# Attention: where the shares of values, the maxima made ahead and the cut of the maxima stand

## The reference

```
x = x + tanh(g) * attention(layernorm(x), context)      # 16 heads of 16 numbers
x = x + tanh(g) * mixture_of_experts(layernorm(x))      # 8 experts, top 2
x = x + tanh(g) * attention(layernorm(x), context)      # again 16 heads
x = x + tanh(g) * (fp8(layernorm(x)) @ fp8(weight).T + bias)
```

## Time and profile before

| what | us |
| --- | --- |
| median of three runs | 1636.0 |
| the profiled execution, its own time | 1635.6 |
| its span, first to last instruction | 1633.6 |
| TensorE matmul busy | 1458.6 (89%) |
| VectorE busy | 1288.9 (79%) |
| ScalarE busy | 1010.4 (62%) |
| GpSimd busy | 636.8 (39%) |
| attention of layer 0, first scores to last values | 115.7 to 439.6 |
| attention of layer 1 | 1203.5 to 1528.3 |
| exponentials, 1024 (L1141) | 550.7 |
| reductions of pairs, 416 (L349) | 488.3 |
| reductions of single banks, 136 (L356) | 87.0 |

### The profile page before, as it was taken

How to read it: one execution, slowest core, us unless ns; L and a number is a source line. 1 busy time by engine, 2 the same in 40 slices (tenths; PEclk the granted TensorE clock), 3 DMA queues, 4 the chain that set the end, 5 groups by cost and what they waited for, 6 DMA issues and landing times. The chain is left out here.

```text
span 1633.6 us, 29384 instructions
## 1 busy us (share of the span) xinstructions
PE 1458.6 (89%) x10909; PEld 950.2 (58%) x10910; DVE 1288.9 (79%) x2135; ACT 1010.4 (62%) x1748; POOL 636.8 (39%) x957
## 2 busy tenths in 40 slices
PE   7989999999994399999999999879979999999845
PEld 6853333333484299999999999745523333333534
DVE  6889999999576766666665564379889999999687
ACT  5648999999741144444444444335549999989544
POOL 4315555556021234443432332255325555553120
PEclk9989999999995599999999999979979999999977
DMA  9974565555262123222222221168845555554103
GB/s 286 329 212 106 128 128 128 128 129 129 74 246 90 46 65 97 65 82 94 71 80 90 75 78 36 45 201 284 250 94 124 129 125 127 126 126 105 35 0 103
DMA packets 118748, 198.64 MB, mean 122 GB/s; under 512 B 29568, under 2 KB 63680, under 8 KB 117584
## 3 DMA queue, kind: packets, MB, share of 16 engines
q1 hardware_dynamic: 83840, 111.22, 22.3%
q0 software_dynamic: 33360, 83.94, 20.6%
q10 hardware_dynamic: 1408, 1.61, 0.3%
HBM read 117.77 MB, written 77.87 MB: 120 GB/s over the span
## 5 line engine op out<-in xcount | busy, mean ns | idle before, releaser
L1141 ACT ACTIVATE i_room<-a_ring 128x512 f32<-128x512 f32 x1024 | 550.7, 606 | 61.7 <-PE a_ring L1077 14.4
L349 DVE TENSOR_REDUCE logit<-a_ring 128x2 f32<-128x1024 f32 x416 | 488.3, 1217 | 3.7 <-PE a_ring L343 3.7
L1088 PE MATMUL a_pout<-i_room,values 128*17 128x256 f32 x4096 | 309.5, 386 | 3.2 <-ACT i_room L1141 1.7
L1799 ACT ACTIVATE e_full<-e_pH,b1T 128x320 f32<-128x320 f32 x256 | 135.0, 527 | 246.4 <-PE e_pH L1740 235.7
L1748 PE MATMUL e_pY<-fc_w,e_hid_hi 128*128 128x512 f32 x640 | 237.2, 407 | 0.5 <-DVE e_hid_lo L1852 0.5
L1077 PE MATMUL a_ring<-i_qk 64*128 64x512 f32 x768 | 193.9, 502 | 19.3 <-DVE logit L349 16.2
L1749 PE MATMUL e_pY<-fc_w,e_hid_lo 128*128 128x256 f32 x640 | 179.8, 281 | 0.0
L1077 PEld LDWEIGHTS a_ring<-i_qk 64*128 64x128 f32 x768 | 72.6, 186 | 183.3 <-DVE logit L349 134.2
L1088 PEld LDWEIGHTS a_pout<-i_room,values 128*17 128x17 f32 x4096 | 74.6, 95 | 175.8 <-ACT i_room L1141 137.1
L1860 POOL DMA_INDIRECT w<-normed,slot_get x80 | 83.6, 1045 | 225.7 <-PE fc_turned L1725 199.6
L1852 DVE TENSOR_TENSOR e_hid_lo<-e_full,e_hid_hi 128x640 fp32r<-128x640 f32 x128 | 119.6, 934 | 55.4 <-ACT e_hid_hi L1808 55.4
(11 more groups left out here) (337 smaller groups left out, 2576.2 us busy)
## 6 DMA issues: line engine op xcount, KB each, us to landing
ks<-i_room SPq DMA_DIRECT2D x64, 256.0 KB, 4.3
outs<-a_osb SPq DMA_DIRECT2D x64, 256.0 KB, 3.4
qs<-i_room SPq DMA_DIRECT2D x60, 256.0 KB, 5.3
fc_raw<-in_L_ffn_fc_w SPq DMA_DIRECT2D x15, 1024.0 KB, 5.4
i_qk<-ks POOLq DMA_DIRECT2D x84, 128.0 KB, 3.4
i_qk<-qs POOLq DMA_DIRECT2D x84, 128.0 KB, 3.6
BIG<-outs SPq DMA_DIRECT2D x64, 128.0 KB
ytok<-r_zeros SPq DMA_DIRECT2D x8, 1024.0 KB, 10.3
```

What stands on the lines that cost most here:

```text
L349: return e.tensor_reduce(nmax[:, :].rearrange("p (x y t) -> p x y t", x=2, y=2)[:, :, p, t], pair[:, :, :], AX.X, ALU.max, negate=True)
L1088: mm = e.matmul(pout[32 * h:32 * h + VW, at], v[:, b * TPB + t, g * HG + h, :], pexp[t][:, h, at], start=(t == 0 and half == 0), stop=(t = ...
L1141: e.activation(pexp[t][:, 2 * p + hh, :], score_bank(n * U + i, hh), ACT.Exp).then_inc(exped, 1)
L1799: e.activation(full[s % 2][:, h * WIDE:(h + 1) * WIDE], pH[h][:, 0:WIDE], ACT.Silu, bias=S.b1T[:, n * KF + f:n * KF + f + 1]).then_inc(act, 1)
```

## The change

Three things, in both layers. (1) Maxima run 16 units ahead, two whole groups, instead of 14; so the stages before an attention make two more units each, and the parts of a group's maxima are due beside the second reduction of the next group. (2) The parts are made in two pieces: the cast behind the next group's first reduction, the difference and the transpose behind its second. (3) Every step has one share of values: unit 5 in step 0, unit 6 in step 1, and unit 7 in step 2, there between the scores and the maxima. ScalarE's copy moves from behind both exponentials of unit 1 to between the two of unit 2.

```diff
-AHEAD = 2 * UNITS - 2
+AHEAD = 2 * UNITS
-LATE_VALUES = (UNITS - 3,), (UNITS - 2, UNITS - 1)
...
                         score_unit(n, i)
+                        if n and i == VALUE_LAG - 1:
+                            values(n - 1, (U - 1) // 2, (U - 1) % 2)
                         if s + 1 < PAIRED:
                             if s:
                                 e.wait_ge(exped, 2 * s - 1)
...
                         elif n and i < VALUE_LAG - 1:
-                            for v_unit in LATE_VALUES[i]:
-                                values(n - 1, v_unit // 2, v_unit % 2)
+                            late = U - VALUE_LAG + i
+                            values(n - 1, late // 2, late % 2)
...
                         for hh in range(2):
                             e.activation(pexp[t][:, 2 * p + hh, :], score_bank(n * U + i, hh), ACT.Exp).then_inc(exped, 1)
-                        if i == 1 and n:
-                            take_outputs(n - 1)
+                            if n and i == VALUE_LAG - 1 and hh == 0:
+                                take_outputs(n - 1)
...
+                def cut_maxima(n, part):
+                    halves, whole = max_halves(nparts[n % 2]), max_whole(nmax[n % 2])
+                    if part == HI:
+                        if (n + 1) * U > AHEAD:
+                            e.wait_ge(reduced, (n + 1) * U - AHEAD)
+                        e.tensor_copy(halves[:, :, 0, :], whole).then_inc(cut, 1)
+                    else:
+                        e.wait_ge(cut, 2 * n - 1)
+                        e.tensor_tensor(halves[:, :, 1, :], whole, halves[:, :, 0, :], ALU.subtract).then_inc(cut, 1)
+
                 def turn_maxima(n):
-                    halves, whole = max_halves(nparts[n % 2]), max_whole(nmax[n % 2])
-                    e.wait_ge(reduced, (n + 1) * U - AHEAD)
-                    e.tensor_copy(halves[:, :, 0, :], whole).then_inc(cut, 1)
-                    e.wait_ge(cut, 2 * n - 1)
-                    e.tensor_tensor(halves[:, :, 1, :], whole, halves[:, :, 0, :], ALU.subtract).then_inc(cut, 1)
                     if n >= 3:
                         e.wait_ge(mrow[(n - 2) % G], moved(n - 2))
                     e.wait_ge(cut, 2 * n)
...
                 for m in range(AHEAD, NG * U):
                     reduce(m)
-                    if m % U == U - 1:
-                        turn_maxima(m // U)
+                    if m >= 2 * U and m % U == 0:
+                        cut_maxima(m // U - 1, HI)
+                    if m >= 2 * U and m % U == 1:
+                        cut_maxima(m // U - 1, LO)
+                        turn_maxima(m // U - 1)
+                for part in (HI, LO):
+                    cut_maxima(NG - 1, part)
+                turn_maxima(NG - 1)
```

## The result

The changed kernel takes **1650.5 us** (median of 4 runs, 1648.2 to 1651.7) against 1635.2 for the kernel before in the same job: ratio 1.0089, 95% interval [1.0077, 1.0101]. On a second chip, later, it took 1646.8 (5 runs) against 1635.4: 1.0074 [1.0061, 1.0087]. So it is slower, by 11 to 15 us, where 8 were predicted. Its profiled execution is 1648.2 us with a span of 1646.1, which is 12.5 over the span of before.

What follows compares the result with a forecast made beforehand. TensorE was taken to set the pace of most steps, waiting for VectorE once a group. Terms 1.9 + 4.5 − 0.4 − 0.3 + 2.4 = +8.1 us on the profiled 1635.6; forecast 1644.0 us, range 1633 to 1651.

Steps and rivals of the forecast that it cites:

- The stall at unit 4: Each group: 2.80 us from T2 (start of scores 2) to T4, where TensorE needs 2.44; 0.36 us stall, +1.9 us overall.
- rival 1: The new stall at unit 4 does not bind and all steps are even: −13.3 us, 1623; chance 0.13.
- rival 2: The stall at unit 4 is smaller, 0.25 or 0.16 us: 1638 or 1632; chance 0.16.
- The cut in two pieces: At scores 3 of each group: the cast no longer waits for the reduction before it, and the old wait is gone.
- the 19.5 us "at stake": Both attentions: period 10.10 against 9.76 for eight even steps, 0.34 us a group, about 58 times.
- The copy: ScalarE's copy between unit 2's exponentials starts at T2 (start of scores 2) + 1.12, ends at 1.72; cost 0.
- Rival 4: Even steps come, but the copy ends late and binds, 0.1 to 0.2 us a group: about 1653; chance 0.04.
- The stages: Ends of the stages before each attention: two more units made, 2 × 1.13 us in each layer, +4.5 us.
- Loads: Twice in each layer a load in which GpSimd pauses lands 0.6 us late for its maxima: 4 × 0.6 = +2.4 us.
- rival 3: Loads late in every group; at a wait of 0.3 us a group, +17 more: 1661; chance 0.07.
- The first group: First group of an attention: the cast leaves the chain before scores 3; −0.3 us (0 to −0.8), in layer 0 alone.
- The tail: End of each attention: two steps lose their maxima, 0.99 instead of 1.22 us; −0.4 taken, at most 0.9 in all.

Runs made afterwards that it cites:

- experiment 4: The kernel before with only the maxima's parts made in two pieces (14 units ahead, old shares and copy): 1632.6 us, ratio 0.9987.
- experiment 7: The kernel before with only the even shares and the copy's new place (14 ahead, parts in one piece): 1639.0 us, ratio 1.0026.
- experiment 3: The changed kernel with the old shares and old copy place, 16 ahead and two pieces kept: 1643.4 us, ratio 1.0044.
- Experiment 9: The changed kernel with both pieces of the maxima's parts one reduction later, still 16 ahead: 1642.0 us, ratio 1.0041.
- experiment 10: The changed kernel with GpSimd's cast of the identity moved behind its last load: 1644.8 us, ratio 1.0052.
- experiment 1: The changed kernel with maxima 14 units ahead again, even shares, copy and two pieces kept: 1639.6 us, ratio 1.0023.
- experiment 8: The kernel before with two pieces and the copy between unit 2's exponentials, 14 ahead, old shares: 1640.0 us, ratio 1.0022.
- experiment 2: The changed kernel with unit 7's share behind the maxima of unit 2 instead of ahead of them: 1643.7 us, ratio 1.0049.

## Why the prediction was right or wrong

The direction and the mechanism were right and the range held the time; the sum was 4.4 us short of the profiled execution's 12.5, and 7 short of the first median. Of the 4.4 the loads are 3.0, the first groups 1.5 and the period 0.9; the stages, the tails and the untouched stages came out 0.3 to 0.4 lower each. The first median lies 0.5 us inside the upper end of the range, which had the loads doubled. Step by step:

**The stall at unit 4, right in place and size.** Predicted 0.43 + 0.56 + 0.54 + 1.22 + 0.05 = 2.80 from T2 to T4; measured 0.42, 0.56, 0.55, then 1.28 to the scores, 2.81. The choice of 0.54 over 0.43 for maxima behind values is what the trace shows (297.06 to 297.61), so the weight load of the maxima is paid openly there, as the rule of the Trainium skill (TensorE: Matmul & The Clock Gate, Part 3, The mechanism) had it. The trace does not bear out the rule's other half. In the kernel before the maxima stand behind scores, which use the same rows of the array, and yet the row of their weight load starts while the scores run, which last from 289.77 to 290.26 (the page also names a background weight buffer, of which no run here tells):

```profile
289.88 0.19 PEld L343 LDWEIGHTS a_ring<-i_qk 64*128 64x128 f32 x2
```

The period came out at 10.13, as predicted, and rivals 1 and 2 fall. The term was 2.8 us for 1.9, since the old period was 10.08 to 10.09 and not 10.10: the mean of the copies had in it one step of layer 1 that was 0.4 us long.

**The cut in two pieces, right but never seen.** Its gain is real, 2.3 us a layer (experiment 4), and the even shares hide all of it (experiment 7). It is also small: with the old shares, once the old wait is gone, the copy behind the double share holds the group at 10.01 us (experiments 3 and 4), far from the 9.76 that the 19.5 us "at stake" were reckoned from.

**The copy, right**: at T2 + 1.12 as worked out (296.08 to 297.20), no wait. Rival 4 falls.

**The stages, right**: +4.2 for +4.5.

**Loads, right in kind, wrong in size**: 5.4 for 2.4. The step that failed is "lands 3.7 later, at 259.2 ... late by 0.6". The row of before was taken over as if landings were a property of the load. They depend on what SyncE issues beside it. The text said that SyncE's DMAs "are issued no later", and took that for harmless; they were issued 0.3 to 0.35 us earlier (3.70 behind scores 7 instead of 4.05), next to the load's last pieces, which then took 4.1 us. A paused load's step lost 1.2 us for the predicted 0.6: 0.4 us and more of the excess is the later landing, and a step loses 0.2 us more than its load is late. Three smaller late steps, 0.7 together, were not foreseen. (The "covered by 2.4 us" was a misreading without effect: 2.4 is the length of the two steps; the room was 1.9.) Experiment 9 shows that moving them away takes the late steps out. The direction of the whole, four late loads, not one in every group, was right, and rival 3 falls.

**The first group, wrong in sign**: "the cast leaves that chain: −0.3", measured +0.6 in each layer. The cast does leave the chain ahead of scores 3, and step 2 is 0.56 us shorter for it in layer 0, within the range given. What the prediction left out is that the cast comes to stand in step 1, beside GpSimd's cast, and is held until that ends: +0.84 in layer 0 and +0.30 in layer 1, by experiment 10. It also left out TensorE's clock, which rose 0.9 and 1.2 us later than before: 0.25 and 0.42 us.

**The tail, right in sign, small**: −0.4 taken, with 0.9 as the most; measured −0.5 in the last steps of the two groups 29 and −0.3 behind them. Against experiment 1, which has the same order of shares, it is the full 0.9.

## What to carry to other kernels

A rearrangement that evens out one engine's steps moves the old peak's neighbours as well: follow the chain from the moved instruction to whoever reads behind it, in this case product, reduction, ring, and price that before counting the evened steps as gained. When several edits come together, measure the square: here a part worth 3 us of the median was in the change and could not be seen. A sum of one engine's times that equals the period does not make that engine the bound: look for its idle time first (experiments 4 and 8). And take a DMA's landing time as a measure of what runs beside it, not as its own: before a transfer's due time is brought forward, ask what other queues issue in its last microseconds.

## What the runs showed of the hardware that was not expected

**A cast on VectorE can be held for as long as an operation of GpSimd lasts.** With both operands in SBUF and 16 elements a partition it takes 0.17 us alone and 1.00 to 1.01 beside GpSimd's cast of 2048 elements (in both layers of the change's two profiles and of experiments 2 and 3), and each time it ends within 0.05 us of GpSimd's end; in experiment 10, where GpSimd runs nothing of that kind, it is 0.17 again. VectorE's reductions from PSUM beside the same operation keep their 1.22. The Trainium skill (SBUF — State Buffer, Who interferes with whom) says that GpSimd and VectorE share one pair of ports, that a cast in VectorE's two-port mode needs it, and that the one that comes second waits for the whole instruction of the other; the trace agrees, though that this cast runs in that mode no run here shows.

**Landing times of the same transfer differ by 1.7 us** (2.4 to 4.1 us for the slower of the last two pieces of a paused load, in experiment 9 and in the change) when VectorE's parts, and with them SyncE's DMAs, come 1.2 us later and nothing else is changed.

**A place in an order can be worth more than its work.** ScalarE's copy costs next to nothing in the gap that the double share leaves and 0.17 us of period one exponential later (experiments 4 and 8), though it waits less there.

**How long the start of a stage runs at the lower clock differs between executions of nearly the same program.** The granted clock rose from 0.50 to 1.00 between 6.9 and 11.4 us behind the first scores of an attention, and the first group's length went with it. In layer 1 of experiment 7, steps 0 to 3 take the same 6.93 us as in the kernel before, but the clock is up after 6.9 us instead of 10.2, and the group takes 11.80 us instead of 13.21.
